# A DLRM interaction tower on one core: pair products in four array strips, a last chunk in halves, splits from PSUM, and a tenth field looked up on chip

## What is computed

```python
e = jnp.stack([tbl_0[ids[:, 0]], ..., tbl_25[ids[:, 25]]], axis=1)
combined = jnp.concatenate([dense_features[:, None, :], e], axis=1)      # 2048 x 27 x 128
interactions = jnp.einsum('bnd,bmd->bnm', combined, combined)
z = jnp.concatenate([dense_features, interactions[:, _TRIU_I, _TRIU_J]], axis=1)
h = jnp.concatenate([z, dense_features], axis=1)                         # 2048 x 607
h = jnp.maximum(h @ W_top1 + b_top1, 0.0)                                # 512
h = jnp.maximum(h @ W_top2 + b_top2, 0.0)                                # 256
y = h @ W_top3
```

## Time and profile before

| | us |
|---|---|
| median of 3 runs | 385.37 |
| lowest, highest | 384.83, 386.34 |
| the profiled execution | 385.82 |
| its span, first to last instruction | 384.0 |
| PE busy (matmuls) | 343.3 |
| POOL busy (gathers) | 262.1 |
| ACT busy | 211.2 |
| DVE busy | 198.8 |

### The profile page before, as it was taken

The page is one execution under the profiler, slowest core; times in us unless marked ns, Lnnn a source line. Parts: engine busy times, 40 slices in busy tenths (PEclk is TensorE's granted clock), DMA queues, the critical chain, the costliest instruction groups (busy, mean ns, idle before and its releaser), DMA issues.

```text
span 384.0 us, 9178 instructions
## 1 busy us (share of the span) xinstructions
PE 343.3 (89%) x3920; PEld 305.5 (80%) x3920; DVE 198.8 (52%) x363; ACT 211.2 (55%) x250; POOL 262.1 (68%) x280
## 2 busy tenths in 40 slices
PE   0567759989999999999899999999999999979986
PEld 0566649977789888998699888998799878968764
DVE  3589853990079604990089505990199306920000
ACT  2257566556644774466635775466645675466222
POOL 6787777777777777777777777777777777770000
PEclk9989989999999999999999999999999999996999
DMA  8996583662257323662267324651266224520410
GB/s 157 255 256 157 153 267 72 158 197 57 56 119 198 108 53 75 166 187 53 56 136 218 72 56 92 164 172 50 56 146 212 67 56 106 127 56 15 91 38 0
DMA packets 51533, 45.44 MB, mean 118 GB/s; under 512 B 35938, under 2 KB 41314, under 8 KB 51494
## 3 DMA queue, kind: packets, MB, share of 16 engines
q1 hardware_dynamic: 42790, 27.02, 28.2%
q0 software_dynamic: 8704, 17.84, 17.9%
HBM read 37.91 MB, written 6.93 MB: 117 GB/s over the span
## 4 chain that ended last, share of the span: by engine, by line
POOL 44%; PE 31%; issue 14%; DMA 7%; SPq 1%; ACT 1%; POOLq 0%
POOL rows L342 44%; PE banks L384 17%; DMA rows<-in_tbl_dram,ids_sb 5%; PE mlp L426 4%; PE moved L367 3%; PE banks L407 3%; PE mlp L436 2%; SPq L252 1%; PE mlp L445 1%; DMA scratch<-products 1%; ACT products L629 1%; DMA features<-scratch 1%; DMA ids_sb<-in_ids_dram 1%; POOLq L104 0%; ACT hidden L661 0%
## 5 line engine op out<-in xcount | busy, mean ns | idle before, releaser
L342 POOL DMA_INDIRECT rows<-in_tbl_dram,ids_sb x272 | 261.1, 960 | 84.0 <-issue 80.8
L539 DVE TENSOR_TENSOR masks<-hot_ids,row_of 125x512 fp32r<-125x512 int32 (+1 forms) x336 | 181.7, 616 | 7.5 <-DMA hot_ids<-in_ids_of_field_dram 4.5
L384 PE MATMUL banks<-masks,high 125*128 125x256 f32 x592 | 151.8, 295 | 17.3 <-DVE low L527 13.6
L384 PE MATMUL banks<-masks,low 125*128 125x256 f32 x592 | 147.0, 286 | 0.0
L384 PEld LDWEIGHTS banks<-masks,high 125*128 125x128 f32 x592 | 115.5, 195 | 21.5 <-issue 16.2
L384 PEld LDWEIGHTS banks<-masks,low 125*128 125x128 f32 x592 | 115.8, 196 | 0.0
L616 ACT ACTIVATE vectors<-moved 128x384 f32<-128x384 f32 (+1 forms) x80 | 87.6, 1095 | 10.9 <-PE moved L367 10.7
L599 ACT ACTIVATE vectors<-banks 128x512 f32<-128x512 f32 (+1 forms) x40 | 44.3, 1107 | 81.7 <-PE banks L384 81.7
L407 PEld LDWEIGHTS banks<-vectors 128*54 128x54 f32 x2048 | 58.7, 136 | 15.9 <-issue 14.0
L629 ACT ACTIVATE products<-banks 118x432 f32<-118x432 f32 x64 | 58.4, 934 | 20.3 <-PE banks L407 19.8
L407 PE MATMUL banks<-vectors 128*54 128x54 f32 x2048 | 65.4, 221 | 0.7 <-issue 0.7
(11 more groups left out here) (22 smaller groups left out, 31.6 us busy)
## 6 DMA issues: line engine op xcount, KB each, us to landing
hot_ids<-in_ids_of_field_dram SPq DMA_DIRECT2D x32, 256.0 KB, 5.2
scratch<-products SPq DMA_DIRECT2D x32, 169.0 KB
rows<-in_tbl_dram,ids_sb POOLq DMA_INDIRECT x272
features<-scratch SPq DMA_DIRECT2D x8, 351.0 KB
scratch<-products SPq DMA_DIRECT2D x32, 42.2 KB
dense_sb<-in_dense_dram SPq DMA_DIRECT2D x8, 128.0 KB, 5.2
hot_ids<-in_ids_of_field_dram SPq DMA_DIRECT2D x8, 128.0 KB, 3.3
vectors<-in_tbl_dram SPq DMA_DIRECT2D x2, 448.0 KB
```

Of the source, the lines that this page charges most:

```text
L342: pool.indirect_dma_start(rows[:, (tile * TILE_ROWS + v) % RING, :], None, tables[f][:, :], bass.IndirectOffsetOnAxis(ap=ids_sb[:, tile, f ...
L384: last = nc.tensor.matmul(banks[:, j % BANKS, m * CHUNK:(m + 1) * CHUNK], part[:, part_of(j * PAIR + m, k), :], masks[:, mask % MASK_RING, ...
L539: nc.vector.tensor_tensor(masks[:, mask % MASK_RING, 0:size], hot_ids[0:PART_ROWS, n % ID_RING, 0:size], row_of[0:PART_ROWS, row:row + 1]. ...
```

## The change

A second table of 1,250 rows is looked up instead of gathered: ten looked up fields in five full pairs, 16 gathered ones in batches of 4. The fifth pair's ten masks are 512 wide.

The pair products are made for one sample at a time, 27 columns, in four strips of 32 array columns; a step has 16 groups of 4 samples, and a chunk 4 steps, one for each of the 4 banks. The order in the chunks is written anew; the layers of a chunk now lie in the following chunk throughout, and a `second_chunk` and a `last_chunk` have orders of their own.

The last chunk's products are written and loaded in two halves, and its layers run per half (`last_layers`). One of its eight second-half writes is issued by ACT. The last layer puts its two halves side by side in two strips, and `store_y` writes two pieces.

At the start, ACT copies each table to two PSUM banks (`copy_table`), and DVE's `split` reads it there; of a table with ten parts the last two are read from SBUF. Splits and masks alternate more finely on DVE.

```diff
-LONGS = [f for f in range(FIELDS) if ROWS[f] == LONG][:1]
+LONGS = [f for f in range(FIELDS) if ROWS[f] == LONG][:2]
...
-STEP_GROUPS = 8
+STEP_GROUPS = 16
...
-BATCH_SIZES = (4, 4, 3, 3, 3)
+BATCH_SIZES = (4, 4, 4, 4)
...
+COPIED_PARTS = 2 * BANK // DIM
...
+        copied = mlp[:, :, :].rearrange("p a b -> p (a b)").rearrange("p (k d) -> p k d", d=DIM)
...
+            def write_last(half):
+                sp.wait_ge(step_kept, LAST * CHUNK_STEPS + (half + 1) * TILE_STEPS)
+                if half == 0:
+                    sp.wait_ge(pairs_loaded, 16 * (LAST - 1))
+
+                for q in range(QUADS if half == 0 else QUADS - 1):
+                    write_quad(sp, LAST, q, scratch_written, half)
...
-            write_products(CHUNKS - 1)
-            load_pairs(CHUNKS - 1)
-            store_y(CHUNKS - 2)
-            store_y(CHUNKS - 1)
-            sp.wait_ge(out_written, 16 * CHUNKS)
+            write_last(0)
+            load_last(0)
+            store_y(LAST - 1)
+            write_last(1)
+            load_last(1)
+            store_last(0)
+            store_last(1)
+            sp.wait_ge(out_written, 16 * HALVES * CHUNKS)
...
                 for g in range(STEP_GROUPS):
                     at = of_tile(c * TILES + t) + (of_step * STEP_GROUPS + g) * QUADS
-                    for couple in range(QUADS // COUPLE):
-                        two = vectors[:, at + couple * COUPLE:at + (couple + 1) * COUPLE, :]\
-                            .rearrange("d s v -> d (s v)")
-                        to = couple * HALF_ARRAY
-                        last = nc.tensor.matmul(banks[to:to + PRODUCT, s % BANKS, g * PRODUCT:(g + 1) * PRODUCT],
-                                                two, two, start=True, stop=True, tile_position=(0, to))
+                    for q in range(QUADS):
+                        one = vectors[:, at + q, :]
+                        to = q * STRIP
+                        last = nc.tensor.matmul(banks[to:to + VECTORS, s, g * VECTORS:(g + 1) * VECTORS],
+                                                one, one, start=True, stop=True, tile_position=(0, to))
...
             def split(h):
                 dve.wait_ge(high_made, h + 1)
-                p = slice(part_of(h, 0), part_of(h, PARTS[h // PAIR]))
-                nc.vector.tensor_tensor(low[:, p, :], stage(h)[0:PART_ROWS, :, :], high[:, p, :].bitcast(fp32),
-                                        ALU.subtract).then_inc(low_made, 1)
+                dve.wait_ge(table_copied, h + 1)
+                for first, last, whole in ((0, COPIED_PARTS, copied), (COPIED_PARTS, PARTS[h // PAIR], stage(h))):
+                    if first < last:
+                        p = slice(part_of(h, first), part_of(h, last))
+                        done = nc.vector.tensor_tensor(low[:, p, :], whole[0:PART_ROWS, first:last, :],
+                                                       high[:, p, :].bitcast(fp32), ALU.subtract)
+                done.then_inc(low_made, 1)
...
+            def copy_table(h):
+                act.wait_ge(table_loaded[h], 32)
+                if h:
+
+                    act.wait_ge(low_made, h)
+                nc.scalar.activation(copied[0:PART_ROWS, :, :], stage(h)[0:PART_ROWS, 0:COPIED_PARTS, :], ACT.Copy)\
+                    .then_inc(table_copied, 1)
```

More of the change, by code:

```diff
@@ L178, in build @@
         scratch_written = sem("scratch_written")
+        last_written = sem("last_written")
         pairs_loaded = sem("pairs_loaded")
+        half_loaded = [sem(f"half_loaded{n}") for n in range(HALVES)]
         first_ready = sem("first_ready")
@@ L200, in of_chunk, with write_quad, groups_of, samples_of @@
                            [list(whole.ap[0]), [1, count], [(second - first) * VECTORS, TILES], [VECTORS, TILE]])
+        def write_quad(engine, c, q, written, half=None):
+            groups = slice(0, CHUNK_GROUPS) if half is None else groups_of(half)
+            at = q * CHUNK_GROUPS if half is None else half * HALF + q * HALF_GROUPS
+            for rows_, columns, slot in (
+                ((0, VECTORS - 1), (0, VECTORS - 1), VECTORS * (WRAP - VECTORS + 1)),
+                ((DELTAS + 1, VECTORS), (VECTORS - DELTAS, VECTORS), (VECTORS + 1) * (DELTAS + 1)),
+            ):
+                height, width = rows_[1] - rows_[0], columns[1] - columns[0]
+                into = bass.AP(scratch[c % 2].tensor, slot * SLOT + at,
+                               [[(VECTORS + 1) * SLOT, height], [VECTORS * SLOT, width],
+                                [1, groups.stop - groups.start]])
+                engine.dma_start(into, products[STRIP * q + rows_[0]:STRIP * q + rows_[1], columns[0]:columns[1], groups])\
+                    .then_inc(written, 16)
+        def groups_of(half):
+            return slice(half * HALF_GROUPS, (half + 1) * HALF_GROUPS)
+        def samples_of(half):
+            return slice(half * HALF, (half + 1) * HALF)
         block = ctx.enter_context(nc.Block())
@@ L442, in last_layer @@
                     return
-                pe.wait_ge(second_kept, MTILES2 * (c + 1))
                 for m in range(MTILES2):
-                    last = nc.tensor.matmul(mlp[0:1, 0, 0:CHUNK], w3_sb[:, m:m + 1], hidden2[:, m, :],
+                    pe.wait_ge(second_kept, MTILES2 * c + m + 1)
+                    for half in range(HALVES):
+                        to = half * STRIP
+                        last = nc.tensor.matmul(mlp[to:to + 1, 0, 0:HALF], w3_sb[:, m:m + 1],
+                                                hidden2[:, m, :].rearrange("d (q g) -> d q g", q=QUADS)[:, :, groups_of(half)],
+                                                start=(m == 0), stop=(m == MTILES2 - 1),
+                                                tile_position=(0, to))
@@ L511, in _ @@
             pe.wait_ge(constants_made, CONSTANTS)
             first_chunk()
-            for i in range(1, CHUNKS):
+            second_chunk()
+            for i in range(2, LAST):
                 chunk(i)
-            for c in (CHUNKS - 2, CHUNKS - 1):
-                for m in range(MTILES1):
-                    first_layer(c, m)
-                for m in range(MTILES2):
-                    second_layer(c, m)
-                last_layer(c)
+            last_chunk()
+            for half in range(HALVES):
+                last_layers(half)
@@ L569, in _ @@
             split(1)
+            split(2)
             for j in range(1, HOT_PAIRS):
-                for m in range(WIDTHS[j]):
-                    split(PAIR * j + m)
-                make_masks(0, j)
+                make_masks(0, j, range(0, 4))
+                split(PAIR * j + 1)
+                make_masks(0, j, range(4, PARTS[j]))
+                if j < HOT_PAIRS - 1:
+                    split(PAIR * j + 2)
             place_dense(0)
@@ L747, in _w1_order @@
+            write_quad(act, LAST, QUADS - 1, last_written, 1)
+            for half in range(HALVES):
+                keep_last(half)
 def _w1_order():
```

324 lines of the change are left out of this document (237 added, 87 removed).

## The result

The changed kernel takes 395.01 us (median of 4 runs, 394.49 to 395.34) against 385.86 for the kernel before in the same session: ratio 1.0238, 95% interval 1.0208 to 1.0268. It is slower by 9 us. I had forecast 369.0, in 359 to 382.

What follows compares the result with a forecast made beforehand. PE and POOL were both taken as nearly full, POOL slower by under a microsecond. Chunk 2 starting at 102.4, five chunks of 40.6 and the tail gave a span of 367.8, so 369.0 us; 8-in-10 range 359 to 382.

Steps and rivals of the forecast that it cites:

- DVE is ready: At the start, DVE's masks and splits, with the new copies to PSUM, were to end at 51.2 us.
- The steady lookups: In a steady chunk, the last mask is ready at 21.9 us and the lookups end at 22.6.
- rival 3: Masks on DVE become the bound: +3 to +3.5 us for each of 5 chunks, 386 us, or 377 if partly; 12%.
- The gathers at the start: POOL's gathers ahead of the loop no longer lose 4.3 us beside the splits; none above 1.3 us except beside two long tables.
- start of chunk 2: Chunk 2 was to start at 102.4 us, against 107.03 before.
- chunks 2 to 6: Five steady chunks of 40.6 us each, PE now behind POOL, so the last chunk starts at 305.4 us.
- the tail: From the last chunk's start at 305.4 us, with halves and chunk 6's layers inside, to 367.8; 2.6 us gained.
- the product step: On PE, 64 matmuls in four strips take 1.04 us, within bounds of 0.81 to 3.34; -3.3 us per chunk.
- The 28 ns a round: Four records, one per strip, take 24 ns plus some 4; 32 such rounds take 0.90 us of a product step.
- Rival 1: Only two strips run at a time: a product step takes 1.9 us, 397 us in all, slower; 9%.
- The bound that I gave: Sign of a wrong forecast: a product step over 1.5 us, or chunks staying at 42 us.
- Rival 2: A floor of 25 ns per record on PE: 3.34 us a product step, 443 us in all; 5%.

Runs made afterwards that it cites:

- spread, without gathers: Changed kernel with product steps some 4 us apart on PE and gathers of all tiles but the first two left out: 374.21 us, ratio 0.9722.
- spread, with gathers: Changed kernel with the same instructions reordered so that product steps stand some 4 us apart on PE: 391.02 us, ratio 1.0137.
- order of the change, without gathers: Changed kernel in its own order, with gathers of all tiles but the first two left out: 383.84 us, ratio 0.9949.
- with pairs: Changed kernel with products back in two strips of 54 columns, half as many matmuls: 381.73 us, ratio 0.9900.
- the run with half the instructions: Changed kernel with products replaced by bfloat16 constants, 27 by 108 columns in one pass, same four strips: 359.05 us, ratio 0.9328.
- 376.08: Kernel before with splits from PSUM and the last chunk in halves with chunk 6's layers inside; nine looked up fields, two strips: 376.08 us, ratio 0.9753.
- the splits: Kernel before with only the splits reading PSUM, a copy on ACT ahead of each: 381.89 us, ratio 0.9894.

## Why the prediction was wrong

Most terms beside the products held. DVE is ready at 51.15 us (forecast 51.2) and the sum of w1 is made at 56.43 to 57.12 (56.8 to 57.5):

```profile
51.15 0.42 DVE L685 COPY vectors<-dense_sb 128x256 f32<-128x256 f32 x1
56.43 0.69 DVE L717 TENSOR_TENSOR w_sb<-w_sb,hidden 128x512 f32<-128x512 f32 x1 [4.86 <-DMA b_sb<-in_b_top_dram]
```

The steady lookups end 22.6 us into the chunk (202.90 to 225.50, forecast 22.6), so rival 3, the masks, did not come. The gathers at the start lost their length. PE's waits for gathered rows left the list. By stretches, with what the product steps took beyond 1.04 us each:

| us | forecast | measured | of this, product steps |
|---|---|---|---|
| start of chunk 2 | 102.4 | 116.5 | +11.8 |
| chunks 2 to 6 | 203.0 | 215.7 | +15.2 |
| from the last chunk's start | 62.4 | 60.3 | +2.2 |

The span missed by 24.7 us and the products by 29.2. So the other terms were together 4.5 us too long, 4.3 of them in the tail, and hid a part of the miss.

**The step that failed is the product step: 1.04 us, -3.3 us per chunk, and the same 4.2 us in chunk 0.** I derived it from the array alone. The 28 ns a round is right for the first 33 records of a step, which start 7 ns apart but for one pause of 28; then they come 17 ns to two, a round of 34 ns, and an undisturbed step is 1.20 us. What sets that second pace was not tested. Summed from start to next over all 32 steps:

| | us |
|---|---|
| forecast, 32 x 1.04 | 33.3 |
| 32 x 1.20, the pace without breaks | 38.4 |
| spread, without gathers | 42.0 |
| spread, with gathers | 56.3 |
| order of the change, without gathers | 50.7 |
| the changed kernel | 62.5 |
| with pairs | 55.6 |

So of the 29.2 us that the products took beyond the forecast, 5.1 are the pace, 12.3 mostly blocks of instructions that came too late (50.7 less 38.4; the eight long breaks of the changed kernel itself make 10.8), and 11.8 the breaks at gathers (62.5 less 50.7; 14.3 in the spread order). The median missed by 26.0. I had counted PE's records, and that they went from 3920 to 6192 was there to be counted; what I never asked is what it costs to bring them. In two strips the same gathers cost nothing that a step shows: a pair of records takes 50 ns, and 64 records take 1.74 us in every chunk. My reading is that a break of 0.25 us is made up there from what PE has already queued; no run shows the queue.

Rival 1 named the number, 1.9 us a step (62.5 / 32 = 1.95) and 397 us, by luck, and the wrong cause: not two strips at a time, but four strips waiting for instructions. The bound that I gave (wrong if a step takes over 1.5 us or chunks stay at 42) was met. Rival 2's floor of 25 ns per record fell: records start 7 ns apart, and 3.5 ns within a round in the run with half the instructions. The Trainium skill, TensorEngine Tiling (Array Packing), section Performance Considerations, counts some 60 cycles of overhead to each matmul; the starts 7 ns apart speak against that as a cost between strips, but its advice not to tile a small dimension further came out right here, for another reason. I had taken its rule per record, 3.34 us a step; per matmul it would be an estimate of 1.6 us (64 x 60 cycles at 2.4 GHz), and the undisturbed 1.20 us lies under that as well.

## What to carry to other kernels

Cutting matmuls into smaller ones also multiplies the instructions, so count them per stretch: in these runs two 16 KB blocks of PE's program never came closer than 3.3 us, and bursts that used them up faster stalled, however free the array was. Look at the instruction queue's line and at PE's "issue" waits before a change that adds records, and test the limit with twice the columns at the same count, and half the count at the same columns. And price each part of a combined change by itself: here a part that cost 13 us and one that cost 4 hid one that gained 4 and the halves of the last chunk. Those were never run alone; 376.08 against the 381.89 of the splits puts them, with their new order, at some 6 us.

## What was not expected of the hardware

- Blocks of PE's program come 4.1 us apart in chunk 0 while gathers run, and 3.5 us apart in the run without later gathers (57.8, 61.3, 64.8 and 68.3 us). That gathers make the difference is not shown: the changed kernel also has two blocks 3.49 us apart with three gathers between them (from 195.41). After a block has landed, a stalled PE went on 1.19 to 1.55 us later.
- In the four strips a gather of POOL breaks PE's stream twice, by 0.21 to 0.31 us, 0.10 to 0.14 us before its start and 0.33 to 0.38 behind it. At 8.5 ns a record that mostly makes 1.20 us into 1.6 to 1.9; at 50 ns for two it shows nowhere.
- Four strips with 54 columns each run as side by side as two (50 ns a round).
- Splits that read PSUM leave the gathers beside them at 947 ns; with splits from SBUF they took up to 2.02 us.
